# The drain between attention and experts: another order for tiles 6 and 7, a shorter inverse root, own scores by halves

## The reference, cut to what matters

```python
x = x + xattn(layernorm(x), ctx, ctx, mask, gamma, beta)  # softmax(q k^T / sqrt(512)) v over 1601 masked context rows,
                                                         # then a layer norm of the result, times gamma, plus beta
x = x + attn(layernorm(x), W_qkv, W_out)                 # every batch of 64 rows attends to itself
xf = layernorm(x).reshape(1024, 512)
scores = xf @ router_w.T                                 # 8 experts
top_v, top_i = top_k(scores, 2); routing_w = softmax(top_v)
for e in range(8):
    out += gelu(xf @ w1[e].T) @ w2[e].T * w_e            # w_e: the row's weight for expert e, 0 if not chosen
x = x + out
```

## Time and profile before

| | before |
|---|---|
| median of 3 runs | 802.03 us (801.93 to 803.76) |
| the profiled execution | 801.91 us, its span 800.3 us |
| PE busy | 740.5 us (93%) |
| DVE busy | 447.5 us (56%) |
| ACT busy | 304.8 us (38%) |
| POOL busy | 148.5 us (19%) |
| HBM traffic | 198.85 MB, mean 248 GB/s |

### The profile page before, as it was taken

How to read it: one execution, slowest core, us unless ns; L and a number is a source line. 1 busy time by engine, 2 the same in 40 slices (tenths; PEclk the granted TensorE clock), 3 DMA queues, 4 the chain that set the end, 5 groups by cost and what they waited for, 6 DMA issues and landing times.

```text
span 800.3 us, 12058 instructions
## 1 busy us (share of the span) xinstructions
PE 740.5 (93%) x4626; PEld 552.3 (69%) x4626; DVE 447.5 (56%) x1052; ACT 304.8 (38%) x508; POOL 148.5 (19%) x160
## 2 busy tenths in 40 slices
PE   5999899999999999862999899999999999999992
PEld 3453345364545453442999899999999998888882
DVE  4153467676868646755456544555556655566520
ACT  2031112122221211221555354556565565656620
POOL 2133030412213010104201021111210212120201
PEclk9999999999999999985899999999999999999997
DMA  9999999999999999211254455564755757674402
GB/s 340 401 421 383 421 384 384 418 379 423 381 421 367 421 412 400 120 52 35 88 163 183 119 176 186 141 208 161 209 189 170 208 205 205 215 235 167 122 1 27
DMA packets 35133, 198.85 MB, mean 248 GB/s; under 512 B 4540, under 2 KB 4924, under 8 KB 14080
## 3 DMA queue, kind: packets, MB, share of 16 engines
q1 hardware_dynamic: 29680, 187.81, 61.8%
q0 software_dynamic: 4672, 9.11, 6.1%
q10 hardware_dynamic: 720, 1.10, 0.4%
HBM read 188.16 MB, written 9.85 MB: 247 GB/s over the span
## 4 chain that ended last, share of the span: by engine, by line
PE 77%; DVE 8%; DMA 7%; issue 3%; SPq 2%; ACT 1%; POOL 1%; POOLq 0%; DVEq 0%; ACTq 0%
PE ps L756 8%; PE ps L985 8%; PE ps L797 8%; PE ps L987 8%; PE ps L986 8%; PE ps L1007 4%; PE ps L1008 4%; PE ps L1009 4%; PE ps L1014 4%; PE ps L1015 4%; PE ps L1016 4%; DMA arena<-in_w_out 3%; DMA arena<-in_ctx_turned 3%; PE ps L812 3%; PE ps L827 3%
## 5 line engine op out<-in xcount | busy, mean ns | idle before, releaser
L459 POOL TENSOR_TENSOR small<-small 128x1 f32<-128x1 f32 x64 | 20.9, 327 | 618.3 <-DVE yb_space L1510 198.0
L987 PE MATMUL ps<-xT,low_a 128*128 128x288 f32 (+5 forms) x384 | 111.1, 289 | 0.0
L1482 DVE TENSOR_TENSOR h_ring<-hid,h_ring 128x288 fp32r<-128x288 f32 (+5 forms) x128 | 55.6, 435 | 96.4 <-ACT h_ring L1173 93.4
L1168 ACT ACTIVATE hid<-ps 128x288 f32<-128x288 f32 (+5 forms) x128 | 50.6, 395 | 151.2 <-PE ps L987 148.7
L797 PE MATMUL ps<-arena 128*64 128x512 f32 (+1 forms) x416 | 94.5, 598 | 3.0 <-DMA arena<-in_ctx 1.8
L1371 DVE TENSOR_TENSOR low_a<-w_raw_a,high_b 128x2048 fp32r<-128x2048 f32 x32 | 73.2, 2291 | 37.7 <-ACT high_b L1108 36.4
L1061 ACT COPY arena<-ps 128x512 f32<-128x512 f32 (+2 forms) x93 | 43.8, 528 | 122.9 <-PE ps L731 66.7
L756 PE MATMUL ps<-arena 128*64 128x512 f32 x384 | 85.5, 596 | 0.9 <-DMA arena<-in_ctx_turned 0.7
L985 PE MATMUL ps<-xT,high_b 128*128 128x288 f32 (+5 forms) x256 | 74.9, 292 | 0.0
L987 PEld LDWEIGHTS ps<-xT,low_a 128*128 128x128 f32 x384 | 73.5, 191 | 0.0
L986 PE MATMUL ps<-xT,high_b 128*128 128x288 f32 (+5 forms) x256 | 73.4, 287 | 0.0
(11 more groups left out here) (192 smaller groups left out, 1615.7 us busy)
## 6 DMA issues: line engine op xcount, KB each, us to landing
arena<-in_ctx_turned SPq DMA_DIRECT2D x48, 1024.0 KB, 23.3
arena<-in_ctx SPq DMA_DIRECT2D x48, 1024.0 KB, 22.7
w_raw_a<-in_w SPq DMA_DIRECT2D x48, 1024.0 KB, 5.0
w_raw_b<-in_w SPq DMA_DIRECT2D x16, 1024.0 KB, 4.9
arena<-in_mask SPq DMA_DIRECT2D x8, 800.5 KB, 26.8
arena<-in_w_qkv SPq DMA_DIRECT2D x3, 1024.0 KB, 9.4
arena<-in_ctx SPq DMA_DIRECT2D x16, 130.0 KB
out<-res SPq DMA_DIRECT2D x8, 256.0 KB, 22.1
```

What stands on the lines that cost most here:

```text
L987: mm = pe.matmul(o, w_low[2 * f][:, cols], high[:, k, 0:w.width], start=False, stop=(k == KC - 1))
L1168: nc.scalar.activation(hid[:, c % 2, 0:w.width], bank(c % UP_BANKS)[:, 0:w.width], ACT.Gelu).then_inc(gelu_done, 1)
L1482: dve.tensor_tensor(h_ring[:, c % RING, 1, 0:w.width], hid[:, c % 2, 0:w.width], h_ring[:, c % RING, 0, 0:w.width].bitcast(F32), ALU.subtr ...
```

## The change

Seven edits:

- PE: `turn_own_probs(7)` and `weigh(7)` stand earlier, in front of `router(6)`; `ranks(6)` stands behind `router(7)`. The list of fills follows.
- DVE: `second_norm(7)` stands in front of `route_first(6)`, and `route_first(7)` in front of `route_second(6)`.
- ACT: the copy of tile 6's turned rows (`xn`, 6) stands behind the casts of weight blocks 0 and 1; the cast of block 3 stands beside that of block 2, in front of the copy of `xr` 7; `gate_exp(6)` behind that copy.
- Routing: the difference of the two best scores is formed at once when the second is known, and signalled (`ratio_set`). The gates are worked out in a function of their own, `gates`, in front of the wait for the ranks; `route_second` is left with four operations. POOL waits for both.
- The inverse root: seven operations. The variance is scaled, the first guess is negative, then one step of third order (three operations) and one Newton step (two).
- Own scores: two products of 64 columns by 64 rows in place of one of 128 by 128, for each of the four chunks.
- Experts: in the last window tile 0's gate waits for its own last matmul, not for that of tile 1.

In `attended` the reciprocal stands in front of the wait for the last sums.

```diff
 fill_order:
-                    ("u", LAST), ("xr", LAST - 1), ("pt", LAST), ("logit", LAST - 1), ("out", LAST),
-                    ("rank", LAST - 1), ("xr", LAST), ("logit", LAST), ("rank", LAST)):
+                    ("u", LAST), ("pt", LAST), ("xr", LAST - 1), ("out", LAST), ("logit", LAST - 1),
+                    ("xr", LAST), ("logit", LAST), ("rank", LAST - 1), ("rank", LAST)):
 send (POOL):
+                pool.wait_ge(gates_ready, t + 1)
                 pool.wait_ge(pos_ready, t + 1)
 own_scores (PE):
                 for k in range(KC):
-                    mm = pe.matmul(o[:, 0:P], gT[:, k, :], xnT[:, k, :], start=(k == 0), stop=(k == KC - 1))
+                    for b in range(2):
+                        q = slice(64 * b, 64 * b + 64)
+                        mm = pe.matmul(o[q, q], gT[:, k, q], xnT[:, k, q], start=(k == 0), stop=(k == KC - 1))
 the drain (PE):
             values(LAST)
+            turn_own_probs(LAST)
             turn_second(LAST - 1)
-            turn_own_probs(LAST)
+            weigh(LAST)
             router(LAST - 1)
-            weigh(LAST)
-            ranks(LAST - 1)
             turn_second(LAST)
             router(LAST)
+            ranks(LAST - 1)
             ranks(LAST)
 down (PE), last window:
+                        if final and w.kind == EXPERTS - 1 and t == 0:
+                            mm.then_inc(first_tile_done, 1)
 the drain (ACT):
             copy_probs(LAST)
-            copy_fill("xn", LAST - 1, xnT, shown=by_chunk)
             gate_exp(LAST - 2)
             for j in range(2):
                 split_high(STATIC[0], j)
+            copy_fill("xn", LAST - 1, xnT, shown=by_chunk)
...
             copy_fill("xr", LAST - 1, xrT, shown=by_chunk)
-            split_high(STATIC[0], 2)
+            for j in range(2, 4):
+                split_high(STATIC[0], j)
+            copy_fill("xr", LAST, xrT, shown=by_chunk)
             gate_exp(LAST - 1)
-            copy_fill("xr", LAST, xrT, shown=by_chunk)
-            split_high(STATIC[0], 3)
             gate_exp(LAST)
 the inverse root (DVE):
+            def rsqrt(variance):
+                own.then_next(dve.tensor_scalar(var, variance, EPS, ROOT_SCALE, ALU.add, ALU.mult))
+                own.then_next(dve.tensor_scalar(rstd.bitcast(I32), var.bitcast(I32), -0.5, GUESS, ALU.mult, ALU.add))
+                own.then_next(dve.scalar_tensor_tensor(out=half, in0=rstd, scalar=rstd, in1=var,
                                                        op0=ALU.mult, op1=ALU.mult))
+                own.then_next(dve.scalar_tensor_tensor(out=half, in0=half, scalar=-10.0 / 3.0, in1=half, ...
+                own.then_next(dve.scalar_tensor_tensor(out=rstd, in0=half, scalar=5.0, in1=rstd, ...
+                own.then_next(dve.scalar_tensor_tensor(out=half, in0=rstd, scalar=rstd, in1=var, ...
+                own.then_next(dve.scalar_tensor_tensor(out=rstd, in0=half, scalar=-64.0 / 3.0, in1=rstd, ...
 routing (DVE):
+            def gates(t):
+                par = t % 2
                 dve.wait_ge(places_free, t + 1)
+                own.then_next(dve.tensor_copy(meta_i[par][:, :, 1], token.to_broadcast([P, TOP_K])))
+                own.then_next(dve.tensor_scalar(token, token, float(P), None, ALU.add))
+                dve.wait_ge(ratio_ready, t + 1)
+                own.then_next(dve.tensor_scalar(low, ratio[par], 1.0, None, ALU.add))
+                own.then_next(dve.reciprocal(meta[par][:, 0, 0:1], low))
+                dve.tensor_tensor(meta[par][:, 1, 0:1], ratio[par], meta[par][:, 0, 0:1], ALU.mult).then_inc(gates_ready, 1)
 route_second, behind rank, product and sum:
-                own.then_next(dve.tensor_copy(pos[par], posf))
...
+                dve.tensor_copy(pos[par], posf).then_inc(pos_ready, 1)
 the drain (DVE):
             copy_pt(LAST)
+            second_norm(LAST)
             route_first(LAST - 1)
-            second_norm(LAST)
+            route_first(LAST)
+            gates(LAST - 1)
             route_second(LAST - 1)
-            route_first(LAST)
+            gates(LAST)
             route_second(LAST)
 gate (DVE), last window:
+                    if w.kind == EXPERTS - 1 and t == 0:
+                        dve.wait_ge(first_tile_done, 1)
```

More of the change, by code:

```diff
@@ L1220, in _ @@
             own = Steps(dve, v_own)
[L1222 to L1230, removed]
-                                                       op0=ALU.mult, op1=ALU.mult))
-                own.then_next(dve.scalar_tensor_tensor(out=rstd, in0=half, scalar=1.5, in1=rstd,
+            def rsqrt(variance):
+                own.then_next(dve.tensor_scalar(var, variance, EPS, ROOT_SCALE, ALU.add, ALU.mult))
+                own.then_next(dve.tensor_scalar(rstd.bitcast(I32), var.bitcast(I32), -0.5, GUESS, ALU.mult, ALU.add))
+                own.then_next(dve.scalar_tensor_tensor(out=half, in0=rstd, scalar=rstd, in1=var,
+                                                       op0=ALU.mult, op1=ALU.mult))
+                own.then_next(dve.scalar_tensor_tensor(out=half, in0=half, scalar=-10.0 / 3.0, in1=half,
+                                                       op0=ALU.add, op1=ALU.mult))
+                own.then_next(dve.scalar_tensor_tensor(out=rstd, in0=half, scalar=5.0, in1=rstd,
+                                                       op0=ALU.add, op1=ALU.mult))
+                own.then_next(dve.scalar_tensor_tensor(out=half, in0=rstd, scalar=rstd, in1=var,
+                                                       op0=ALU.mult, op1=ALU.mult))
+                own.then_next(dve.scalar_tensor_tensor(out=rstd, in0=half, scalar=-64.0 / 3.0, in1=rstd,
                                                        op0=ALU.add, op1=ALU.mult))
@@ L1244, in normalize @@
                 moments(src)
-                rsqrt_start(var, mv[:, 1:2])
-                for _ in range(NEWTON):
-                    rsqrt_step(var)
+                rsqrt(mv[:, 1:2])
                 return dve.tensor_scalar(dst, src, mv[:, 0:1], rstd, ALU.subtract, ALU.mult)
@@ L1278, in attended @@
             def attended(j):
+                dve.wait_ge(exp_done, j + 1)
+                own.then_next(dve.reciprocal(inv, rowsum[:, j % 2:j % 2 + 1]))
                 dve.wait_ge(pv_block, j * NBLK + NBLK)
                 moments(bank(NBLK - 1))
-                own.then_next(dve.reciprocal(inv, rowsum[:, j % 2:j % 2 + 1]))
                 own.then_next(dve.tensor_scalar(var, mv[:, 1:2], inv, inv, ALU.mult, ALU.mult))
-                rsqrt_start(var, var)
-                for _ in range(NEWTON):
-                    rsqrt_step(var)
+                rsqrt(var)
                 own.then_next(dve.tensor_tensor(rstd, rstd, inv, ALU.mult))
@@ L1335, in route_first @@
                     own.then_next(dve.tensor_reduce(best[:, n:n + 1], src, AX.X, ALU.max))
+                    if n == 1:
+                        dve.tensor_tensor(ratio[par], best[:, 1:2], best[:, 0:1], ALU.subtract).then_inc(ratio_set, 1)
                     own.then_next(dve.scalar_tensor_tensor(out=tmp, in0=src, scalar=best[:, n:n + 1], in1=expert_key,
@@ L1343, in route_first @@
                         src = logit2
-                own.then_next(dve.tensor_tensor(ratio[par], best[:, 1:2], best[:, 0:1], ALU.subtract))
                 own.then_next(dve.tensor_tensor(both[par], pick[par][0], pick[par][1], ALU.add))
                 dve.tensor_tensor(cum[t + 1], cum[t], both[par], ALU.add).then_inc(picked, 1)
+            def gates(t):
+                par = t % 2
+                dve.wait_ge(places_free, t + 1)
+                own.then_next(dve.tensor_copy(meta_i[par][:, :, 1], token.to_broadcast([P, TOP_K])))
[4 more added lines that the diff above has]
+                dve.tensor_tensor(meta[par][:, 1, 0:1], ratio[par], meta[par][:, 0, 0:1], ALU.mult).then_inc(gates_ready, 1)
             def route_second(t):
                 par = t % 2
-                dve.wait_ge(places_free, t + 1)
                 dve.wait_ge(filled, filled_at("rank", t))
@@ L1398, in _ @@
                 if runs(r - 3):
+                    gates(r - 3)
                     route_second(r - 3)
@@ L1411, in _ @@
                 split_low(STATIC[0], j)
+            gates(LAST - 2)
             route_second(LAST - 2)
```

21 lines of the change are left out of this document (8 added, 13 removed).

## The result

The kernel after took 797.69 us as a median of 6 runs (796.77 to 799.14), before on the same chip 801.98 (801.79 to 803.76, 6 runs): ratio 0.9944, interval 0.9931 to 0.9958. It is 4.3 us faster. I had forecast 8.6, and the time lies outside my range (791.2 to 796.9).

A forecast was written before the change was run, and what follows sets the result against it. PE was taken to bound the loop, with DMA close behind, and a DVE-then-POOL latency chain the drain; gains of 3.2 (loop), 4.7 (drain) and 0.7 (end) sum to 8.6, giving a median of 793.4 us, range 791.2 to 796.9.

The forecast's parts named there:

- The root: Inverse root on DVE: seven operations take 1.48 us, not 1.92; gain 0.44 whenever a root is on the chain.
- Own scores: PE in the loop: halved products gain 0.42 by starts or 0.53 by durations; 0.5 taken, in five turns, 2.5.
- The end: Behind the last matmul: tile 0's gate and POOL's first scatter start 0.7 us earlier; gain 0.7.
- step 8: Drain, POOL: send(7) waits for POOL's own queue, starting at 362.95; first fetch at 366.96, gain 4.66.
- the drain's 4.66: Drain: gather, turned rows and start of the experts all come 4.66 us earlier.
- rival on the port: Drain: DVE's subtraction starts before POOL's addition ahead of send(7), which then waits 2.2 us: 795.6; chance 0.18.
- If the addition waits for both, 797.8: Worse form of the rival on the port: POOL's addition waits for both DVE subtractions; 797.8 us, no separate chance.
- the single wait: Milder form of the rival on the port: send(7) waits 2.2 us for one subtraction; 795.6, chance 0.18.
- Step 5: Drain: with weigh(7) ahead of tile 6's router, second_norm(7) starts at 346.8, not 353.77: 6.97 us earlier.
- step 1: Start of drain: three roots bring route_first(5) 1.33 us earlier; with the early difference, casts of blocks 0, 1 2.46 earlier.
- the loop, 3.2: Loop gain of 3.2 us: 2.5 from own scores in five turns, 0.7 more from DVE in turn 3.
- clock-holds rival: Drain: clock not yet fallen, tile 7's turning takes 0.60 not 1.11, router shorter too; 792.3 us, chance 0.08.

The follow-up runs named there:

- e15: Kernel after with the old order of the drain on PE, DVE and ACT, other edits kept; 793.30 us, ratio 0.9897.
- e13: Kernel after with DVE's subtractions of weight blocks 2 and 3 moved clear of POOL's whole send(7), ACT casting both blocks earlier; 795.02 us, ratio 0.9921.
- e10: Kernel before with only the inverse root in seven operations; 798.55 us, ratio 0.9966.
- e3: Kernel after with the gates ahead of the softmax in the loop; 796.25 us, ratio 0.9930.
- e11: Kernel before with only the new order of the drain on PE, DVE and ACT; 804.08 us, ratio 1.0028.
- e12: Kernel before with only ACT's casts of weight blocks 0 and 1 ahead of its copy of xn 6; 801.62 us, ratio 1.0002.
- e6: Kernel before with only the last window's tile 0 gated on its own last matmul; 801.21 us, ratio 0.9994.
- e1: Kernel after with DVE's subtractions of weight blocks 2 and 3 held until POOL's second addition for send(7) is done; 796.72 us, ratio 0.9936.
- e2: Kernel after with POOL's small wait-carrying additions replaced by memsets, except in the part for more than 8 windows; 795.83 us, ratio 0.9921.
- e16: e15 with the gates ahead of the softmax in the loop; 792.18 us, ratio 0.9886.

## Why the prediction was wrong

**Right.** Up to send(6) the drain ran as the table has it, each step within 0.6 of the forecast. The root takes 1.46 (313.90 - 312.44; forecast 1.48). Own scores bring 0.43 a turn: the difference by starts (0.42), not by durations (0.53) or the 0.5 that I took. The end brought 0.80 for 0.7.

**Wrong: the port in step 8, "DVE has its places ready at about 360.7 and POOL's own queue is late: send(7) at 362.95."** Send(7) stood 59.05 behind out(5) and its addition ended only at 61.30, 3.6 later than forecast (57.66). Of the drain's 4.66 it left 1.34, since the rest of the chain then ran 0.3 faster. The cause was my rival on the port, in its form "If the addition waits for both, 797.8"; measured 797.7. That the two numbers agree so well is luck, since the loop missed as well. I gave the rival 0.18 and the single wait, though "The two lie within 0.2 of each other"; what waited were two additions, each for one subtraction.

Two intervals decided it. POOL needed 4.14 from send(6) to places_kept(7), not 3.81, since its scatter comes 0.67 and not 0.34 behind its addition at send(6) (0.67 to 0.69 in every run with the second wait, gates_ready, in between, 0.34 in every run without). And DVE's small operations follow closer where they don't depend on one another (the second gates start 0.08 behind the last cast of the first tile), so the subtractions stood 3.85 behind send(6), not 4.25 (363.2 - 358.95). places_kept(7) was to come 0.44 ahead of the subtractions (4.25 - 3.81) and came 0.29 behind the first (3.85 - 4.14).

**Wrong beside it: what the gain was put down to.** Step 5 has second_norm(7) 6.97 earlier, 3.2 of it by the new order (6.97 - 3.76). It came 6.83 earlier, and 3.35 earlier than in e15, so that step holds. But I never worked out the old order with the other edits. There (e15) send(6) is not kept behind route_first(7) and goes out at 50.2; POOL is free at 54.5, DVE ready at 57.0. In the new order send(6) goes at 52.9 and POOL can't start send(7) before 57.2 (e13: 360.04 - 302.50 = 57.5). So even with the lock away the order brings nothing, and with it 3.7 are lost.

What shortens the drain are the roots, own scores of tile 7 and, in the last step, the gates: from route_first(7) to send(7) 5.82 in before, 5.83 in e10, 4.71 in e15. I had called the gates "worth nothing there"; in the old order they are worth 1.1. Another 1.1 lies ahead of the casts of blocks 0 and 1: they start 2.45 earlier against out(5), of which three roots make 1.33, and the rest is the difference of the scores, formed earlier. I had both in step 1; no run has the early difference alone.

**Wrong by a size: the loop, 3.2.** It brought 2.36 in after's profile, 4.28 in e15's and 4.50 in e3's. Of e15's 4.28, 2.6 are own scores (six by 0.43), 1.2 the wait of turn 3, for which I had 0.7, and 0.5 lie ahead of the first own scores (108.59 and 108.04), which I had at nothing. Such a difference of two profiles is not sure to better than 0.7: with the loop of before, out(5) stands at 305.48 in before, 305.44 in e11, 305.25 in e12 and 304.73 in e6. What took turn 3's gain away in after was a lock again, met by the gates' cast. I had looked at the mask operation in turn 3 only, not at where the moved operations would meet it in the next ones.

**Experts, 0.60, forecast 0.** No work changed there. The window below is 4 us at 0.96 of the full clock in after and at 0.50 in before: before's experts ran their first 5.4 us at the half clock, after's 4.3. Half of that difference, 0.5, is nearly all of the 0.60.
```profile
382.66:386.66 4.00, 4.00 (x18) 4.00 (x18) 0.14 (x1) 1.02 (x3) 3.17 (x6) 0.50 0.53 156
```
```profile
382.66:386.66 4.00, 4.00 (x31) 0.96 0.12 36
```
The first is before's with all engines, the second after's with PE alone. The clock-holds rival came true in part, by chance: the granted clock of after is 0.94 from 348 to 349 and 0.50 behind it, so the turning of tile 7 took 0.70 and the router behind it 1.88. From second_norm(7) to route_first(7) that is 7.10, where I had 7.6. In e1 and e2 the turning took 1.11.

Still open is how much of e15's spread (791.39 to 795.46) is the loop's chance meeting and how much the clock.

## What to carry to other kernels

Before you credit a new order of work with a gain, work out the old order with all the other edits: a chain that two engines share moves its bound, and the shorter pieces may have won it already. Where VectorE's large two-input operations and GpSimd's small ones come within a few tenths of each other, take the collision as the case, price every GpSimd instruction in the stretch (indirect scatters too), and put the large operation where GpSimd has nothing to do. Small operations that are moved in a loop have to be placed against every long operation of the other engine, turn by turn; a cast that meets the mask operation is held 1.5 longer here than a product.

## What the runs showed of the hardware

- Beside VectorE's subtraction of two SBUF inputs (2.25): a GpSimd addition was held until its end (2.04 to 2.32 for 0.19), a memset not (0.10), and an indirect scatter of 0.98 took 1.87 to 2.75, until 0.8 to 0.9 behind the end of the subtraction. A scatter that had started 0.34 ahead of the subtraction (e15) took its usual 0.96.
- VectorE's operations that meet GpSimd's 5.63 mask operation are held for one of two lengths, and their kind decides. Operations with two SBUF inputs (sums, products, the steps of the root) came free 4.1 to 4.2 us behind its start, casts only at its end, 5.6 to 5.7 behind its start. That is so in all 14 profiles, whether the operation started with the mask operation or later. The two pairs of rows from turn 4 show it: the cast of after ends at 181.47, 5.66 behind the start, the product of e15 at 179.88, 4.14 behind it. So the lock lasts for the whole instruction, as the prediction has it, only for one kind. Why the other comes free sooner no run shows.
- In the first window of the experts PE waits 3.24, and the clock falls to half a second time: for 3.4 us in after, for 6.8 in e16 by its windows of 2 us below (the fall of each from 1.00, doubled, times 2 us; the one left out has 0.50). From the first matmul behind this wait to the last of the kernel it is 339.9 to 340.0 in the eight profiles with the short fall and 341.0 to 341.2 in the six with the long one: the long one costs 1.1.
```profile
434.00:436.00 2.00, 1.00 (x4) 1.04 (x5) 2.00 (x5) 0.52 (x1) 0.00 (x0) 0.53 0.04 16
436.00:438.00 2.00, 2.00 (x9) 2.00 (x9) 1.45 (x1) 0.00 (x0) 0.00 (x0) 0.50 0.00 0
...
440.00:442.00 2.00, 2.00 (x13) 2.00 (x12) 0.00 (x0) 0.50 (x2) 0.00 (x0) 0.77 0.00 0
```
- In 3 of the 14 profiled executions the clock also fell to half early in the drain, during the sums of tile 7: for some 3.4 us in e3 (from about 309.8) and e10 (from about 313.4), for some 6.8 in e6 (from about 313.1). tops(6) came 1.7 later in e3 than in after and 2.2 later in e6 than in before; for e10 I estimate 1.0, from the 1.77 that four roots should have given and the 0.80 that they gave. The waits of PE ahead of these sums, 0.8 in e3 and e10 and 1.2 in e6, stand in the other profiles as well, without a fall; what decides is open.
